# A four-part graph network on one core: typed layers in one block each, pair counts fetched early, clone search moved, and a pair stage with fewer waits and wider copies

## The reference

```python
x = layernorm(x + arma_network(x, src, dst, ...))      # two ARMA layers: 3 stacks, 2 steps, 128->256->128
x = layernorm(x + gcn(x, src, dst, W, b))              # one sum over edges and self loops
x = layernorm(x + rgcn(x, src, dst, edge_type, ...))   # two typed layers
x = layernorm(x + neighbour(x, src, dst, ...))         # one plain sum over edges

def rgcn(...):                                         # both directions of each edge: 18 segments a node
    for l in range(2):
        agg = segment_sum(output[srcs], seg, 18 * n).reshape(18, n, 128)
        hidden = output @ W[l, 18] + b[l, 18]
        for r in range(9):
            for inv in (0, 1):
                s = r + 9 * inv
                hidden = 2.0 * (hidden + agg[s] @ W[l, s] + count[s] * b[l, s]) / max(count[s], 1)
        output = relu(hidden) if l == 0 else hidden
```

## Time and profile before

| | us |
|---|---|
| runs | 4264.36, 4268.54, 4275.59: median 4268.54 |
| the profiled execution: its own time / its span | 4261.65 / 4260.4 |
| busy: PE, DVE, POOL, ACT | 3151.3, 2177.2, 1996.6, 1410.3 |
| granted TensorE clock, mean | 0.78 |

### The profile page before, as it was taken

One profiled execution on the slowest core, in us unless ns is written; L12 is line 12 of the kernel. 1 busy time (PEld: TensorE's weight loads), 2 busy tenths in 40 slices (PEclk: granted clock), 3 DMA queues, 4 the chain that ended last, 5 costly groups with the idle time before them and its releaser, 6 DMA issues. The chain is left out here.

```text
span 4260.4 us, 54185 instructions
## 1 busy us (share of the span) xinstructions
PE 3151.3 (74%) x15552; PEld 2507.9 (59%) x15554; DVE 2177.2 (51%) x3834; ACT 1410.3 (33%) x2732; POOL 1996.6 (47%) x2227
## 2 busy tenths in 40 slices
PE   6878665899999799998966878767683544444459
PEld 3545322779999596996735767655552533333348
DVE  8979996425544651556655555434363422222224
ACT  5949575556666663665200000000000000000015
POOL 4727221111111010110276777777756777777751
PEclk8989898999999899999985565555586855555559
DMA  4000156558888392984562222222263222222226
GB/s 168 5 1 1 51 200 200 204 191 293 290 290 286 136 309 92 315 286 175 197 235 67 54 54 53 53 53 54 53 242 122 53 53 53 53 53 53 53 67 209
DMA packets 170983, 572.68 MB, mean 134 GB/s; under 512 B 54368, under 2 KB 63937, under 8 KB 170380
## 3 DMA queue, kind: packets, MB, share of 16 engines
q1 hardware_dynamic: 90838, 396.53, 27.1%
q0 software_dynamic: 79536, 172.73, 14.0%
q10 hardware_dynamic: 390, 0.60, 0.0%
HBM read 405.92 MB, written 163.77 MB: 134 GB/s over the span
## 5 line engine op out<-in xcount | busy, mean ns | idle before, releaser
L2070 PE MATMUL ps_sum_rgcn<-gathered_rgcn,select_sum_rgcn 128*128 x3328 | 971.1, 439 | 570.3 <-SPq L1961 513.5
L2070 PEld LDWEIGHTS ps_sum_rgcn<-gathered_rgcn,select_sum_rgcn 128*128 128x128 f32 x3328 | 760.3, 307 | 637.0 <-issue 635.5
L1650 PE MATMUL ps_sum_arma<-pair_counts_f_sum_arma,parts_sum_arma 128*128 128x448 f32 (+1 forms) x3850 | 852.3, 373 | 14.3 <-ACT pair_counts_f_sum_arma L1691 13.6
L1986 POOL DMA_INDIRECT gathered_rgcn<-by_dst,row x782 | 739.1, 945 | 238.3 <-issue 214.9
L1650 PEld LDWEIGHTS ps_sum_arma<-pair_counts_f_sum_arma,parts_sum_arma 128*128 128x128 f32 x3850 | 708.3, 190 | 68.4 <-issue 15.1
L1986 POOL DMA_INDIRECT gathered_rgcn<-by_src,row x558 | 527.3, 945 | 199.4 <-issue 156.0
L2107 ACT COPY acc_rgcn<-ps_sum_rgcn 128x128 f32<-128x128 f32 x100 | 26.6, 266 | 1640.3 <-PE ps_sum_rgcn L2070 1640.3
L1529 POOL DMA_DIRECT2D rows<-parts_sum_arma x275 | 152.5, 555 | 884.9 <-DVE parts_sum_arma L1738 840.6
L2144 DVE TENSOR_TENSOR select_sum_rgcn<-one_hot_sum_rgcn,ps_coef_sum_rgcn 128x2048 f32<-128x2048 bf16 x52 | 118.9, 2287 | 575.6 <-PE ps_sum_rgcn L2070 575.5
L531 POOL DMA_INDIRECT scattered_rows<-record_sorts,to_row_sorts x254 | 244.0, 960 | 191.0 <-POOLq L199 114.2
L1995 PE MATMUL ps_turn_sum_rgcn<-ident,one_hot_sum_rgcn 128*128 128x128 bf16 x832 | 244.3, 301 | 79.3 <-DVE one_hot_sum_rgcn L2116 51.6
(11 more groups left out here) (466 smaller groups left out, 5132.5 us busy)
## 6 DMA issues: line engine op xcount, KB each, us to landing
blocks_arma_mid<-pairs SPq DMA_DIRECT2D x125, 800.0 KB, 6.3
axT_arma<-pairs SPq DMA_DIRECT2D x100, 800.0 KB, 6.2
pair_counts_arma_sum<-pairs SPq DMA_DIRECT2D x50, 800.0 KB, 6.2
rows<-parts_sum_arma POOLq DMA_DIRECT2D x275, 128.0 KB, 5.5
by_src<-rows_rgcn_tables SPq DMA_DIRECT2D x50, 576.0 KB, 3.8
by_dst<-rows_rgcn_tables SPq DMA_DIRECT2D x50, 576.0 KB, 3.6
exact<-whole_pairs SPq DMA_DIRECT2D x25, 800.0 KB, 3.3
pairs<-whole_pairs POOLq DMA_DIRECT2D x25, 800.0 KB, 5.2
```

The source lines that it names most:

```text
L1650: last = nc.tensor.matmul(ps[:, g, 0:here.stop - here.start], half(part), counts[:, n % 2, here].bitcast(F32R), start=t == 0 and part == 0 ...
L1986: nc.gpsimd.indirect_dma_start(got[:, n % PLACES, :], None, table, bass.IndirectOffsetOnAxis(ap=o.row[:, n % C:n % C + 1], axis=0)).then_i ...
L2070: nc.tensor.matmul(ps[:, bass.ds(slot, P)], select[:, parity, u, :], rows[:, bass.ds(place, D)], start=False, stop=False, skip_group_check ...
```

## The change

1. Load: only the last tile of `xcur` is cleared, and the stage's end no longer waits for x; SP waits for it (`x_loaded`) ahead of the fill of `by_src` in the next stage.
2. Staircase: the search for heavy nodes and clones and the work for `need` are taken out; the store `loop` is put here, on SP, whose block waits for its landing. `end_of` and the free counts of `item_at` count *rooms* of two spans, 4 a tile (`ROOMS`), with three small VectorE operations more.
3. Pair stage: the hardware loop is written out; 24 buffers for `target`; VectorE waits for TensorE once in 8 items; ScalarE copies and clears by rooms; SP fetches the first 4 tiles of `pairs` into a ring that `sum_x` goes on to use; nothing waits for the last stores here: `sum_x` waits for `kept` before each fetch, and GpSimd for all stores before the clone gathers.
4. `sum_x`: the search runs here, in pieces beside the tiles (VectorE at n = 2, 4, 5 to 9, 11; TensorE after tiles 3 and 10), the clone gathers behind GpSimd's row store 11, `clone_rest` at tile 14, its store at tile 17, and the pieces of `factors` from tile 14 on.
5. Typed layers: `typed_tables_stage` and `typed_sum_stage` become `typed_layer_stage`, one block a layer. The table rows, and later `select`, `turned` and `mine`, share SBUF, the stages' PSUM is one room. GpSimd's gathers run on from the 112 to the rest. The turn back of layer 0 is the start of layer 1's block, on TensorE and ScalarE; that of layer 1 stays a stage.

```diff
@@ load_stage
-            sp.wait_ge(loaded, 16 * 5)
+            sp.wait_ge(loaded, 16 * 3)
-            nc.vector.memset(k.xcur[:, :, :], 0.0).then_inc(zeroed, 1)
+            nc.vector.memset(k.xcur[:, NT - 1, :], 0.0).then_inc(zeroed, 1)
@@ rank_stage
+                sp.wait_ge(k.x_loaded, 32)
@@ staircase_stage
+        @block.sync
+        def _(sp):
+            with nc.allow_non_contiguous_dma(reason="one value per node"):
+                sp.dma_start(loop.rearrange("(t p) o -> p (t o)", p=P), k.dinv_loop[:, :]).then_inc(looped, 16)
+            sp.wait_ge(looped, 16)
...
+            then(nc.vector.tensor_scalar(room_i[:, :, :], fourths(tile_at), 2.0, None, ALU.add))
+            then(nc.vector.tensor_single_scalar(room_i[:, :, :], room_i[:, :, :], 1, ALU.arith_shift_right))
+            then(nc.vector.scalar_tensor_tensor(q.item_at[:, :, DOZEN:DOZEN + DOZEN // FOUR], fourths(tile_i), float(ROOMS),
+                                                room_i[:, :, :], ALU.mult, ALU.add))
@@ pair_counts_stage
+    AHEAD = V + V // 2
-        target = c.sb("target_one_hot", [P, V, SPAN], FP16)
+        target = c.sb("target_one_hot", [P, AHEAD, SPAN], FP16)
             for n in range(ITEMS):
-                dve.wait_ge(multiplied, n + 1)
+                if n % (V // 2) == 0 and n > V:
+                    dve.wait_ge(multiplied, n)
...
-            with pe.Fori(0, ITEMS // BODY) as i:
-                for u in range(BODY):
...
+            for n in range(ITEMS):
+                if n % DOZEN == 0:
+                    table = load(PE, item_at, n // DOZEN * ROW, ROW, (SPANS - 1) * SPAN)
...
-                for g in range(SPANS):
-                    act.wait_ge(multiplied, ends[g] if i * SPANS + g < BLOCKS_OF_PAIRS - 1 else ITEMS + V)
+                for g in range(ROOMS):
+                    act.wait_ge(multiplied, ends[g] if i * ROOMS + g < NT * ROOMS - 1 else ITEMS + V)
...
                 sp.dma_start(exact[i * P:i * P + P, :], whole[:, i % 2, :]).then_inc(stored[i % 2], 16)
-            for n in (0, 1):
-                sp.wait_ge(stored[n], 16 * len(range(n, NT, 2)))
-                sp.wait_ge(kept[n], 16 * len(range(n, NT, 2)))
+                if J <= i < J + FETCHED:
+                    n = i - J
+                    sp.wait_ge(kept[n % 2], 16 * (n // 2 + 1))
+                    sp.dma_start(ring[:, n, :], halves[n * P:n * P + P, :]).then_inc(k.prefetched, 16)
@@ dense_stage
-    CLONED = 9
+    CLONED = 17
+    READY, COUNTED, FILLED, NODED, RESTED = 2, 4, 5, 11, 14
...
-                at = bass.IndirectOffsetOnAxis(ap=k.clone_node[:, 0:1], axis=0)
-                nc.gpsimd.indirect_dma_start(clone_whole[:, :], None, exact[:, :], at).then_inc(k.cloned, 16)
-                nc.gpsimd.indirect_dma_start(clone_half[:, :], None, pairs[:, :], at).then_inc(k.cloned, 16)
...
+                    if exact is not None and t == NODED:
+                        gp.wait_ge(noded, 1)
+                        for n in (0, 1):
+                            gp.wait_ge(k.exact_kept[n], 16 * len(range(n, NT, 2)))
+                            gp.wait_ge(k.kept[n], 16 * len(range(n, NT, 2)))
+                        at = bass.IndirectOffsetOnAxis(ap=k.clone_node[:, 0:1], axis=0)
+                        nc.gpsimd.indirect_dma_start(clone_whole[:, :], None, exact[:, :], at).then_inc(k.cloned, 16)
+                        nc.gpsimd.indirect_dma_start(clone_half[:, :], None, pairs[:, :], at).then_inc(k.cloned, 16)
...
+                if exact is not None and n >= FETCHED:
+                    sp.wait_ge(k.kept[n % 2], 16 * (n // 2 + 1))
+                if exact is None or n >= FETCHED:
+                    sp.dma_start(ring[n % RING], pairs[t * P:t * P + P, :]).then_inc(streamed[n % RING], 16)
...
-                if n >= RING:
+                if n >= (RESTED if exact is not None else RING):
                     next(apart, None)
                     next(apart, None)
@@ typed_layer_stage, gpsimd
+            gp.wait_ge(tiled, NT)
+            for n in range(BEHIND, TOTAL * U):
                 if not fetched(n):
                     continue
+                if n == C:
+                    gp.wait_ge(tiled, TILES)
@@ typed_layer_stage, tensor, ahead of the tables' matmuls
+            if turned_from is not None:
+                for t in range(NT):
+                    last = nc.tensor.transpose(room[:, t // 4, t % 4 * P:t % 4 * P + P], acc[:, t, :], k.ident[:, :])
+                    if t % 4 == 3 or t == NT - 1:
+                        last.then_inc(flopped, 1)
@@ rgcn_layer
-        for layer, xT in ((0, k.xT[:, :]), (1, hidden)):
-            typed_tables_stage(nc, k, f"rgcn_tables{layer}", xT, [dram["by_src"], dram["by_dst"]], got, acc)
-            typed_sum_stage(nc, k, f"sum_rgcn{layer}", typed, got, acc, layer == 0,
-                            loads=() if layer else typed_loads(k, A, 1))
-            turn_back_stage(nc, k, f"rgcn_back{layer}", acc, hidden, ACT.Copy if layer else ACT.Relu)
+        typed_layer_stage(nc, k, "sum_rgcn0", k.xT[:, :], tables, got, acc, True, loads=typed_loads(k, A, 1))
+        typed_layer_stage(nc, k, "sum_rgcn1", hidden, tables, got, acc, False, turned_from=ACT.Relu)
+        turn_back_stage(nc, k, "rgcn_back1", acc, hidden, ACT.Copy)
```

More of the change, by code:

```diff
@@ L53 @@
 F32R = mybir.dt.float32r
+FETCHED = 4
+ROOMS = -(-SPANS // 2)
 BLOCKS_OF_PAIRS = NT * SPANS
@@ L59 @@
 LOW = 32
+TWO_P = 2 * P
 TWO = LOW + NT
@@ L1984, in _ @@
                         nc.gpsimd.nop(nofuse=True)
[L1985 to L1989 removed]
+                gather(n)
         @block.tensor
@@ L2184, in _ @@
                 heat(U, 1)
+            for j in range(J):
+                dve.wait_ge(stored[j], 16 * (TILES // J))
+            if find:
                 for g in range(3):
```

464 lines of the change are left out of this document (244 added, 220 removed).

## The result

| | us |
|---|---|
| before, 4 runs | 4264.36 to 4275.59, median 4267.18 |
| the changed kernel, 4 runs | 4237.18 to 4244.95, median 4241.68 |
| ratio | 0.9936, 95% interval 0.9919 to 0.9953 |
| the profiled execution: own time / span | 4244.95 / 4243.6 |

What follows compares the result with a forecast made beforehand. No engine bounds the whole; GpSimd's gather issue bounds the typed layers, VectorE the pair stage. Terms -4.9 - 3.6 - 7 - 9.6 - 5.5 - 32 = -62.6 gave 4205 us, range 4181 to 4228.

Steps and rivals of the forecast that it cites:

- Load, -4.9: Load stage: ends at 10.2 in place of 15.18 us, with a shorter memset and x no longer waited for.
- so all moves 2.5 up: Load stage: SP's zeros wait for the memsets, so a shorter memset moves their issue's end from 12.19 to 9.7.
- Staircase, -3.6: Staircase: without the search the next stage starts at 493.5, not 497.14; the store `loop` is taken as hidden.
- Pair stage, -7: Pair stage: of VectorE's 8.2 us idle, 7 go, as buffers and wide copies cover TensorE's stops; ends 0 and -28.
- Waits per eight: Pair stage: VectorE's waits as such were taken to cost nothing, so fewer waits save only idle time.
- the first rival: Pair stage: VectorE without waits runs faster and TensorE becomes the bound; 20 us more saved, 4185; 12%.
- End of the stage, -9.6: Pair stage's end: the first matmuls of `sum_x` come at 710.5 in place of 720.12 us.
- TensorE needs the barrier, 0.5: Pair stage's end: after the last issue TensorE needs 0.53 + 0.5 us for the barrier, then a split and one cast.
- `sum_x`, -5.5: `sum_x`: 17 us to gain at a steady pace, less payments given as 11.6, including a clone wait of 4.5 to 8.
- Typed layers, -32: Typed layers: gaps between GpSimd's gathers go, -20.5 in layer 0, -10.5 in layer 1, -1 at the border.
- The third rival: Typed layers: they give half, as the gap at 2325.53 stays; 12 to 16 us less saved, 4220; 10%.
- The fourth: Pair stage: fetching TensorE's written-out straight code holds it up and the kernel gets slower, 4284; 2%.

Runs made afterwards that it cites:

- e10: The changed kernel with x fetched by SP at the start of the next stage, not in the load stage: 4242.3 us, first rank operation at 9.97.
- e1: The changed kernel with rooms of one span again, all else as changed: 4202.1 us, pair stage 201.8.
- e5: The changed kernel with wide rooms kept, but ScalarE clears each room right behind its own copy: 4214.5 us, pair stage 204.2.
- e6: The changed kernel without the stores of `exact` in the pair stage, the clone correction left out: 4212.6 us, pair stage 199.0.
- e8: The kernel before with the typed layers' part of the change alone: 4226.5 us, pair stage 206.7.
- e2: The changed kernel with TensorE's hardware loop of 96 items again, wide rooms and 24 buffers kept: 4269.9 us, pair stage 250.1.
- e9: The changed kernel with rooms of one span and TensorE's hardware loop, 24 buffers and waits per eight kept: 4230.8 us, pair stage 219.8.
- e3: The changed kernel with 16 target buffers and VectorE's wait before each item again: 4236.0 us, pair stage 234.7.
- e7: The changed kernel with GpSimd's last store of `pairs` issued at the start of `sum_x`, not at the pair stage's end: 4250.7 us.
- e11: The changed kernel with rooms of one span once more, timed: median 4205.5 us, ratio to the kernel before 0.9868.
- e4: The changed kernel with rooms of one span, hardware loop, 16 buffers and a wait each, early fetches kept: 4224.9 us, pair stage 211.6.

## Why the prediction was wrong, step by step

- **Load, -4.9: half came** (-2.05). The step "so all moves 2.5 up" failed: the zeros waited for SP's issue of x, not for the memsets (e10). What came is the wait for x's landing.
- **Staircase, -3.6: right** (-3.8), `loop` hidden: it landed 18.0 us behind its issue, at 488.2, where half of 28.3 had been guessed.
- **Pair stage, -7: the step that failed.** It said that ScalarE's wide copies "cover TensorE's stops", and its ends, 0 and -28, left no room for a loss. I had counted ScalarE's busy time, which did fall (163.3 to 152.2), and not when a room comes free. That could be read in the code: each room is cleared only behind the copy of the next one, at some 0.5 us an operation (163.32 us for 349). Doubled in length (1.03 and 1.02 us), and with four rooms in place of seven, TensorE's lead falls from five spans to a room and a bit. It cost 34.5 us (e1), and e5 shows that the rooms cost this only with the late clears; e6 shows that the long register loads have a part in it too. Without it the step would have been right in size: 201.8 is 8.8 under before, and 4.9 under the same code in e8. But that gain is not where I put it: with 24 buffers the straight code, which I had priced at nothing, gives 14 us (e2) and 18 (e9), and e9 gives the buffers no gain of their own with the loop. The prediction's row of a stop for ScalarE's clear, 0.84 us ahead of a dozen, is not one of these: it ended 0.48 us behind a load of 1.10, in the view of its line at that time:

```profile
L1228 PEldq TENSOR_LOAD <-item_at_adjacency x1: 1102/1102/1102, 647.7 to 647.7; - x1
```

- **Waits per eight: right** in size. They cost VectorE 2 to 8 ns each (e1, e3), near "nothing"; the first rival's 20 us didn't come. The Trainium skill ("VectorE: DVE Perf Modes", "The DRAIN you can't avoid") says that a semaphore after each operation adds nothing to a run of them. No run here tests that: the change keeps every semaphore and takes away waits, and these cost at most 5 us in 576 operations.
- **End of the stage, -9.6: half** (-4.4). The step "TensorE needs the barrier, 0.5" failed: GpSimd's drain of 6.17 us stood behind SP's wait in the kernel before as well, and stayed (e7).
- **`sum_x`, -5.5: right** (-5.1), with a slip in its sum: the payments listed come to 10.6, not 11.6. The clone wait was 7.75, in the range of 4.5 to 8; the gather took 10.7 us to land, nearer to the row's 13.6 than to the 3.9 estimated beside it.
- **Typed layers, -32: right** (-32.5), shown alone by e8. The third rival fell.
- **Rivals.** The fourth had the right stage and the right sign for it, a slower TensorE stream, but the wrong cause: straight code helps. No rival was the wide rooms. The three terms that missed did so by 33, 5 and 3 us. That e11 lands on 4205.5, the forecast, is chance: its load and barrier gave 8 less and the pair stage 2 more, and the kernel before was 8 us faster in its runs, so that it saved 53.6 us and not 63.

## What to carry to other kernels

Before an operation is made wider to save fixed cost, count the buffers between the two engines: ask when each one comes free, and how much work the producer has until it needs it. Half the operations at twice the length can leave an engine less busy and the engine behind it waiting, and where two engines are within a few per cent of each other, each wait shows in full. A wait that is removed at a barrier gives only the distance to the next one that ends there: look for the drains of all five engines.

## What the runs showed of the hardware

- A `TENSOR_LOAD` of 16 values to TensorE's registers took 1.10 us with idle DMA queues and up to 4.3 with stores under way; without SP's stores the median fell from 1.88 to 1.11 us (e6). The next matmul started 0.35 us behind the load's end in straight code, 0.45 in the loop. ScalarE's loads of `end_of`, once a tile, were not alike either: 0.31 us for 4 values (the changed kernel), 0.55 for 8 (before), but 1.63 in the median for 7, in rows of 7 (e1, and as much in e4, which so differ from the kernel before in this too). Why isn't shown. The three rows, changed kernel, before and e1:

```profile
L1079 ACTq TENSOR_LOAD <-end_of_adjacency x25: 305/309/521, 495.3 to 717.5; - x25
```

```profile
L1228 ACTq TENSOR_LOAD <-end_of_adjacency x25: 543/546/764, 498.0 to 697.6; - x25
```

```profile
L1078 ACTq TENSOR_LOAD <-end_of_adjacency x25: 961/1633/2354, 492.5 to 684.5; - x25
```

- GpSimd reached a barrier only when its own last DMA had landed: a drain of 6.17 us behind an 800 KB store, which ended 1.0 to 1.1 us behind the landing (before, changed kernel, e7). SP's drain behind the same size took 0.12.
- TensorE's granted clock was 0.83 in two slices of 10 us with two stops each, 0.75 to 0.96 us and 2.6 us, with 4 matmuls between them: part of the time at 1.2 GHz, the rest at 2.4. In e5 a stop of 3.11 us left 12 matmuls behind it at 2.76 us, and one of 3.45 us was followed by 24 in 6.75; in the kernel before one of 2.01 us was followed by 24 in 7.04. The pair stage's mean was 0.88 in the changed kernel, 0.94 in e1 and e5. What exactly the clock follows isn't settled here.
- In the same stage, with 24 buffers, the hardware loop was 14 to 18 us slower than 576 items written out; the loads' sums were about equal (93.1 and 95.6 us with wide rooms, 90.1 and 86.2 with rooms of one span).
